# Attention scores over 32-row groups of TensorE and probabilities turned by transposing transfers

## The reference

```python
scale = 384 ** -0.5
q = (x @ Wq.T).reshape(b, n, 12, 32)
k = (x @ Wk.T).reshape(b, n, 12, 32)
v = (x @ Wv.T + bv).reshape(b, n, 12, 32)
scores = einsum('bqhd,bkhd->bhqk', q, k) * scale + (adj + adj)[:, None]
p = softmax(scores)                      # rows of zeros give 0
out = einsum('bhqk,bkhd->bqhd', p, v).reshape(b, n, 384)
return out @ Wo.T + bo
```

## Time and profile before

| | us |
|---|---|
| median of 3 runs | 1612.74 |
| lowest to highest | 1612.06 to 1613.54 |
| the profiled execution | 1610.95 |
| its span, first to last instruction | 1608.7 |
| PE busy | 1530.1 |
| DVE busy | 1247.8 |
| ACT busy | 900.9 |
| POOL busy | 470.3 |

### The profile page before, as it was taken

The page is one execution under the profiler, slowest core; times in us unless marked ns, Lnnn a source line. Parts: engine busy times, 40 slices in busy tenths (PEclk is TensorE's granted clock), DMA queues, the critical chain, the costliest instruction groups (busy, mean ns, idle before and its releaser), DMA issues.

```text
span 1608.7 us, 38829 instructions
## 1 busy us (share of the span) xinstructions
PE 1530.1 (95%) x13760; PEld 1501.6 (93%) x13760; DVE 1247.8 (78%) x4559; ACT 900.9 (56%) x2091; POOL 470.3 (29%) x926
## 2 busy tenths in 40 slices
PE   4799999999999999999999999999999999999984
PEld 4799999999999999999999999999999999999973
DVE  6568887778887777888777888777788877788753
ACT  4556566556556555656655665655565665566531
POOL 4113332233323223333223332313333322332222
PEclk8799999999999999999999999999999999999986
DMA  8222022222112222212222211222221222221100
GB/s 246 61 63 71 31 51 73 70 73 73 49 39 63 74 70 73 67 30 55 74 70 73 73 44 44 64 71 72 73 65 30 57 73 70 74 73 35 40 10 10
DMA packets 84637, 101.66 MB, mean 63 GB/s; under 512 B 6640, under 2 KB 84208, under 8 KB 84448
## 3 DMA queue, kind: packets, MB, share of 16 engines
q1 hardware_dynamic: 83872, 98.20, 22.6%
q0 software_dynamic: 576, 0.99, 0.3%
HBM read 61.41 MB, written 37.75 MB: 62 GB/s over the span
## 4 chain that ended last, share of the span: by engine, by line
PE 90%; ACT 5%; DVE 2%; issue 1%; DMA 1%; POOL 1%; SPq 0%; DVEq 0%; ACTq 0%; POOLq 0%
PE bank L355 72%; PE bank L430 5%; PE bank L361 4%; PE bank L423 3%; PE bank L414 3%; ACT c_sb L556 3%; PE bank L436 1%; ACT qk L495 1%; PE bank L448 0%; DMA pT<-w 0%; DMA k<-qk_parts 0%; ACT prob L519 0%; DMA x_sb<-x 0%; DVE c_sb L645 0%; DVE weights L582 0%
## 5 line engine op out<-in xcount | busy, mean ns | idle before, releaser
L355 PE MATMUL bank<-h,weights 128*128 128x256 f32 x3456 | 429.8, 282 | 5.4 <-DVE h L758 5.0
L355 PEld LDWEIGHTS bank<-h,weights 128*128 128x128 f32 x3456 | 412.4, 190 | 6.4 <-issue 5.7
L519 ACT ACTIVATE prob<-prob,rmin 128x128 f32<-128x128 f32 x768 | 240.3, 390 | 13.3 <-DVE rmin L675 13.3
L355 PE MATMUL bank<-weights,h 128*128 128x384 f32 x1152 | 228.7, 343 | 0.0
L355 PE MATMUL bank<-hA,weights 128*128 128x256 f32 x1728 | 218.8, 281 | 1.5 <-DVE hA L606 1.5
L606 DVE TENSOR_TENSOR n<-bank,n 128x512 fp32r<-128x512 f32 x192 | 128.5, 683 | 109.9 <-ACT n L495 109.8
L355 PEld LDWEIGHTS bank<-hA,weights 128*128 128x128 f32 x1728 | 210.9, 189 | 1.9 <-DVE hA L606 1.9
L355 PEld LDWEIGHTS bank<-weights,h 128*128 128x128 f32 x1152 | 193.9, 188 | 0.0
L817 POOL TENSOR_SCALAR less_mean_gnn<-mv_gnn 128x2 f32<-128x2 f32 x64 | 14.4, 225 | 582.0 <-DVE mv_gnn L611 582.0
L495 ACT ACTIVATE n<-bank 128x512 fp32r<-128x512 f32 x192 | 113.9, 594 | 117.6 <-PE bank L355 117.6
L675 DVE CUSTOM_DVE_ANT_0 prob<-bank,adj_sb 128x128 f32<-128x128 f32 x768 | 174.5, 286 | 0.1
(11 more groups left out here) (109 smaller groups left out, 2660.3 us busy)
## 6 DMA issues: line engine op xcount, KB each, us to landing
qk_parts<-qk SPq DMA_DIRECT2D x96, 256.0 KB, 2.4
q<-qk_parts SPq DMA_DIRECT2D x96, 192.0 KB, 4.6
k<-qk_parts SPq DMA_DIRECT2D x96, 192.0 KB, 5.5
x_sb<-x SPq DMA_DIRECT2D x32, 384.0 KB, 4.1
out<-x SPq DMA_DIRECT2D x32, 384.0 KB, 2.5
adj_sb<-adj SPq DMA_DIRECT2D x32, 128.0 KB, 2.1
prob<-w SPq DMA_DIRECT2D x4, 576.0 KB, 7.2
x<-w SPq DMA_DIRECT2D x3, 576.0 KB, 4.8
```

The source lines that it names most:

```text
L355: mm = pe.matmul(out, lhsT, rhs, start=(n == 0), stop=(n == len(pairs) - 1))
L519: e = act.activation(prob[:, j, h, :], prob[:, j, h, :], ACT.Exp, bias=rmin[:, j, h:h + 1], scale=-1.0)
```

## The change

- `q3`, `k3`, `qk_dram` and the steps qs and stack are gone. A score is now a product of 32 rows, read straight from `qk`, which holds two groups. The four heads of a chunk lie on the four row groups of the array, and the three parts are three products that add up in PSUM. S is now numbered by row group a instead of chunk: bank `Sja` gets the three heads a, 4 + a, 8 + a. All 36 products of a graph are issued in one step (`last == HC - 1`), in the order chunk, part, row group; the other S steps on PE only wait for their bank.
- The P steps are gone from PE, and their banks. `prob` holds one graph. ACT copies the high part of three heads in fp16 to a new tile `pp` (`ph`), DVE subtracts it from `prob` into its low half (`pl`), and SP turns three 128x128 blocks at a time from `pp` to `pT` (`pth`, `ptl`): 16 transfers a group. The same waits on PV0 and PV1 stand ahead of them.
- `xn1` has a tile of its own. `BANK` and `ORDER` are new for all engines: PV1 and its followers come late in a round, OT1 and WO1 in the next.

```diff
     "SP": [
-        ("k3", 1), ("ld_adj", 2), ("out", -1), ("qs0", 2), ("qs1", 2), ("qs2", 2), ("ld_x", 3), ("q3", 2)],
+        ("ld_x", 2), ("pth01", 1), ("pth03", 1), ("pth00", 1), ("pth02", 1), ("ptl01", 1), ("ptl03", 1), ("ptl02", 1),
+        ("ptl00", 1), ("ld_adj", 2), ("pth13", 1), ("pth11", 1), ("pth10", 1), ("ptl13", 1), ("ptl10", 1), ("ptl11", 1),
+        ("ptl12", 1), ("pth12", 1), ("out", -1)],
...
-        qk = sb("qk", [P, 2, 2 * C, T], F16)
+        qk = sb("qk", [P, 2, 2, 2 * C, T], F16)
+        xn1 = sb("xn1", [P, G, H])
         v2 = sb("v2", [P, 2, G, NH, DA], F16)
-        prob = sb("prob", [P, G, NH, P])
+        prob = sb("prob", [P, NH, P])
+        pp = sb("prob_parts", [P, 2, NH, P], F16)
         pT = sb("pT", [P, 2, NH, P], F16)
...
+                elif step[:2] == "pt":
+                    part, j, a = "hl".index(step[2]), int(step[3]), int(step[4])
+                    hs = slice(a * C, (a + 1) * C)
+                    if g == 0:
+                        sp.wait_ge(s_wlo, NW)
+                    sp.wait_ge(s_part[part][a], G * g + j + 1)
+                    if j == 0:
+                        wait_filled(sp, "PV1", g - 1)
                     else:
+                        wait_filled(sp, "PV0", g)
+                    sp.dma_start_transpose(pT[:, part, hs, :], pp[:, part, hs, :].rearrange("p h q -> p (h q)")).then_inc(s_turned[part][a], 16)
...
                 elif step[0] == "S":
-                    for a in range(HC):
-                        mm = pe.matmul(bank(step)[:, a * P:(a + 1) * P], q3[:, a * C + c, j * P:(j + 1) * P], k3[:, a * C + c, j * P:(j + 1) * P], start=True, stop=True)
-                    mm.then_inc(full(step), 1)
+                    j, last = int(step[1]), int(step[2])
+                    if last == HC - 1:
+                        for k in range(3):
+                            wait_drained(pe, f"QK{k}", g)
+                        js = slice(j * P, (j + 1) * P)
+                        for c in range(C):
+                            for n, (u, v) in enumerate(PARTS):
+                                for a in range(HC):
+                                    rs = slice(a * D, (a + 1) * D)
+                                    mm = pe.matmul(bank(f"S{j}{a}")[:, c * P:(c + 1) * P], qk[rs, g % 2, u, c, js], qk[rs, g % 2, v, C + c, js],
+                                                   start=(n == 0), stop=(n == len(PARTS) - 1))
+                                    if (c, n) == (C - 1, len(PARTS) - 1):
+                                        mm.then_inc(full(f"S{j}{a}"), 1)
                 elif step[:2] == "PV":
                     j = int(step[2])
                     wait_drained(pe, f"V{j}", g)
-                    for c in range(C):
-                        wait_drained(pe, f"P{j}{c}", g)
+                    for part in (HI, LO):
+                        for a in range(HC):
+                            pe.wait_ge(s_turned[part][a], 16 * (G * g + j + 1))
...
-                    for a in range(HC):
-                        mm = pe.transpose(bank(step)[:, a * P:(a + 1) * P], prob[:, j, c * HC + a, :], ident[:, :])
...
+                elif step[:2] == "ph":
+                    j, a = int(step[2]), int(step[3])
+                    act.wait_ge(s_exp[j][a], g + 1)
+                    ge(act, s_turned[HI][a], 16 * (G * g + j))
+                    act.activation(pp[:, HI, a * C:(a + 1) * C, :], prob[:, a:NH:HC, :], ACT.Copy).then_inc(s_part[HI][a], 1)
...
-                elif step[0] == "P":
-                    j, c = int(step[1]), int(step[2])
-                    hs = slice(c * HC, (c + 1) * HC)
-                    lo(step, g, pT[:, LO, hs, :], pT[:, HI, hs, :], HC * P, "p (h q) -> p h q", h=HC)
+                elif step[:2] == "pl":
+                    j, a = int(step[2]), int(step[3])
+                    hs = slice(a * C, (a + 1) * C)
+                    dve.wait_ge(s_part[HI][a], G * g + j + 1)
+                    ge(dve, s_turned[LO][a], 16 * (G * g + j))
+                    dve.tensor_tensor(pp[:, LO, hs, :], prob[:, a:NH:HC, :], pp[:, HI, hs, :], ALU.subtract).then_inc(s_part[LO][a], 1)
```

More of the change, by code:

```diff
@@ L71 @@
 BANK = {
[L72 to L79, removed]
+    0: ["N10", "U1", "S03", "N02", "T1b", "QK0"],
+    1: ["V0", "S12", "C01"],
+    2: ["N11", "T2b", "HL11", "HL00", "PV0", "PV1"],
+    3: ["OT1", "S02", "S10"],
+    4: ["HTa", "T2a", "N01", "S13", "HL01", "OT0"],
+    5: ["HL10", "S01", "C10", "AT", "T1a", "QK1", "WO0"],
+    6: ["HTb", "WO1", "N12", "N00", "U0", "QK2"],
+    7: ["S00", "C11", "S11", "C00", "V1"],
 }
@@ L83 @@
     "SP": [
[1 row of a table removed]
[3 rows of a table added]
     "PE": [
[5 rows of a table removed]
-    "ACT": [
[5 rows of a table removed]
-        ("HTb", 0)],
-    "DVE": [
[9 rows of a table removed]
[5 rows of a table added]
+    "ACT": [
[6 rows of a table added]
+    "DVE": [
[9 rows of a table added]
     "POOL": [
-        ("ln1", 2), ("ml", 0), ("gn1", -1), ("mu", 0), ("za0", -1), ("za1", -1), ("zb0", -1), ("xbo1", 2), ("xbo0", 2),
-        ("zb1", -1), ("gn0", 0), ("ln2", 1)],
-}
-SPLIT_JOBS = (["T1a", "T1b", "QK0", "QK1", "QK2", "V0", "V1"] + [f"P{j}{c}" for j in range(G) for c in range(C)] +
-              ["OT0", "OT1", "T2a", "T2b"] + [f"N{l}{k}" for l in range(L) for k in range(3)] +
+        ("ln2", 0), ("ln1", 2), ("xbo1", 2), ("xbo0", 2), ("ml", 0), ("gn1", -1), ("mu", 0), ("za0", -1), ("za1", -1),
+        ("zb0", -1), ("zb1", -1), ("gn0", 0)],
+}
+SPLIT_JOBS = (["T1a", "T1b", "QK0", "QK1", "QK2", "V0", "V1",
+              "OT0", "OT1", "T2a", "T2b"] + [f"N{l}{k}" for l in range(L) for k in range(3)] +
               [f"HL{l}{j}" for l in range(L) for j in range(G)])
@@ L218, in build @@
         s_xbo = [sem(f"x_plus_bo{j}") for j in range(G)]
-        s_q3, s_k3 = sem("q3_in"), sem("k3_in")
-        s_qs = [sem(f"qk_out{k}") for k in range(3)]
-        s_exp = [[sem(f"exps{j}{c}") for c in range(C)] for j in range(G)]
+        s_exp = [[sem(f"exps{j}{a}") for a in range(HC)] for j in range(G)]
+        s_part = [[sem(f"prob_{n}{a}") for a in range(HC)] for n in ("hi", "lo")]
+        s_turned = [[sem(f"prob_turned_{n}{a}") for a in range(HC)] for n in ("hi", "lo")]
         s_stats = {k: sem(f"stats_{k}") for k in ("ln1", "ln2")}
@@ L300, in load_weights @@
                     sp.dma_start(staged(m), w_d[m].rearrange("(c p) o -> p c o", p=P)).then_inc(s_wload[STAGE_OF[m]], 16)
-            def stack(dst, s, which, parts, p):
-                for r, part in enumerate(parts):
-                    heads = qk_dram[p, :, part, which * C:which * C + C, :].rearrange("(a d) c t -> d a (c t)", d=D)
-                    sp.dma_start(dst[D * r:D * r + D, :, :].rearrange("d (a c) t -> d a (c t)", a=HC), heads).then_inc(s, 16)
             def run(step, g):
@@ L418, in run @@
                     wait_drained(pe, f"V{j}", g)
-                    for c in range(C):
-                        wait_drained(pe, f"P{j}{c}", g)
+                    for part in (HI, LO):
+                        for a in range(HC):
+                            pe.wait_ge(s_turned[part][a], 16 * (G * g + j + 1))
                     for h in range(NH):
                         for n, (a, b) in enumerate(PARTS):
-                            mm = pe.matmul(bank(step)[:, h * DA:(h + 1) * DA], pT[:, a, h, :], v2[:, b, j, h, :],
+                            mm = pe.matmul(bank(step)[:, h * DA:(h + 1) * DA], pT[:, a, h % HC * C + h // HC, :], v2[:, b, j, h, :],
                                            start=(h == 0 and n == 0), stop=(n == 2), skip_group_check=True)
-                    mm.then_inc(full(step), 1)
-                elif step[0] == "P":
-                    j, c = int(step[1]), int(step[2])
-                    pe.wait_ge(s_exp[j][c], g + 1)
-                    for a in range(HC):
-                        mm = pe.transpose(bank(step)[:, a * P:(a + 1) * P], prob[:, j, c * HC + a, :], ident[:, :])
                     mm.then_inc(full(step), 1)
@@ L501, in run @@
                     act.wait_ge(s_ln["ln1"], g + 1)
-                    for k in range(3):
-                        ge(act, s_qs[k], 16 * g)
                     act.activation(xn1[:, j, :], x_sb[:, p, j, :], ACT.Relu, bias=shift["ln1"][:, j:j + 1], scale=scale["ln1"][:, j:j + 1]).then_inc(s_xn1[j], 1)
@@ L666, in run @@
                 elif step[0] == "S":
-                    j, c = int(step[1]), int(step[2])
+                    j, a = int(step[1]), int(step[2])
                     dve.wait_ge(s_adjin[p], 16 * (n + 1))
@@ L670, in run @@
                         dve.wait_ge(s_wlo, 8)
+                    ge(dve, s_part[LO][a], G * g + j)
                     wait_filled(dve, step, g)
-                    take_wait(3 + j * C + c)
-                    for a in range(HC):
+                    take_wait(3 + j * HC + a)
+                    for c in range(C):
                         h = c * HC + a
```

(6 more changed lines are left out.)

59 lines of the change are left out of this document (14 added, 45 removed), and 39 rows, old and new, of the table ORDER.

## The result

The changed kernel takes **1,723.5 us** (median of four runs, 1,721.2 to 1,726.4) against 1,613.1 us before on the same chip (four runs, 1,612.1 to 1,614.5). The ratio is **1.069, interval 1.067 to 1.070**: slower by 110 us, where 1,554 us and a gain of 59 were forecast. The time lies inside the range, on the side of rival 1, and the direction came out the other way.

A forecast was written before the change was run, and what follows sets the result against it. PE, busy 95% with hardly a gap, was taken as the bound. 1,610.95 us, -67 for PE's products, +8 for the ends, 1.8 for the median gave 1,554 us; range 1,528 to 1,760, the forecast's own 1,528 to 1,600.

The forecast's parts named there:

- rival 1: SP's queue before PV0 and PV1: transposing transfers too slow, gain gone at 1.13 us each, 1,675 us at 1.25; chance 0.32.
- t = 0.8 us: SP's queue: time one transposing transfer takes it, 0.42 us issue plus 0.36 us bytes, bounded by 0.42 and 1.66.
- 8t + L: Eight transfers before PV0 or PV1 plus the last one's tail: 8.5 us, fitting the covers, so no steady wait.
- The packet argument for rival 1: Transfers on SP's queue: 384 packets each, 24 per engine at 69 ns, giving 1.66 us a transfer.
- The landing, L = 2.1: Tail of the last transposing transfer before PV0 or PV1, taken from the adj load: 2.1 us.
- The covers of 9.5 and 10.9 us: PE's work that hides the transfers: 9.5 us between PV0 and PV1, 10.9 us from the first copies to PV0.
- Score products at 0.0253 us: 72 new 32-row products a group on PE, priced like PV's: +1.82 us; ends 0.0135 (side by side) and 0.054 each.
- Rival 2: Score products on PE: row groups don't overlap, 0.054 us each eats the whole gain, 1,620 us; chance 0.08.
- Removing the transposes and the old score products: PE, per group: 24 transposes of P go, -2.61 us, and 24 score products over 96 rows, -1.29 us.
- The swap of waits: PE: 0.3 us of wait appears at WO0 and about as much goes at HTb; counted as even.
- Rival 3: DVE's new subtractions from two SBUF tensors held up by POOL: 1.5 to 2.5 us on PE, 1,618 us; chance 0.08.
- The ends, +8 us: Filling and draining: nothing covers the first group's transfer chain; +8 us, 0 to 15.

The follow-up runs named there:

- plain_copy: The changed kernel with its 512 transposing transfers replaced by plain copies of the same size, output not the reference's: 1,549.5 us, ratio 0.961.
- six_blocks: The changed kernel with 8 transposing transfers of six blocks a group instead of 16 of three, whole computation kept: 1,551.2 us, ratio 0.962.
- six_serial: six_blocks with the score products issued row group by row group instead of in turn over the four: 1,596.3 us, ratio 0.989.

## Why the prediction went wrong, step by step

- **What bounds the kernel before: right.** PE with hardly a gap set the time, and in the two kernels without regular waits at PV (plain_copy, six_blocks) it sets it again, at 94% busy and a period of 45.56 and 45.50 us. The forecast was 45.5, though by two errors that cancel (below).
- **The failed step: t = 0.8 us for a transposing transfer.** It was built as 0.42 (a plain issue) plus 0.36 (98 KB at the rate of the plain queue). Measured: 1.21 us of issue and 1.30 from one to the next. Both halves were wrong in kind. The issue of a transposing transfer isn't that of a plain one (0.50 here), and the bytes add nothing to it, since SP is free again before they have moved. The bounds, 0.42 and 1.66, held the value, and rival 1 named the place, the formula and the break-even at t = 1.13, which lies under 1.30. What was missing was weight: the cover was exceeded by a value in the middle of the bounds, and 0.32 was too little for it. So the step "8t + L = 8.5 us, inside the covers, no wait" failed; the rows show 12.8 us from PV0 to PV1 and 4.26 us of wait a group.
- **The packet argument for rival 1** reached its number by a wrong road. Transfers do have 384 packets, but 69 ns a packet, taken from large rows, doesn't carry over: the packets of 256 bytes take 20 ns of an engine each (247 us of sixteen engines for 196,608).
- **The landing, L = 2.1: right** (2.3). **The covers of 9.5 and 10.9 us: right**; the rows above show 9.4 us at the first and, from the first issue for graph 0 at 804.72 to the end of PE's work at 815.47, 10.75 at the second. The formula of the waits is near the measurement (5.0 and 4.26 us a group), in part by luck: an issue counted twice stands for the handovers and the long issues.
- **Score products at 0.0253 us: too dear.** They take 0.017 with all around them, so 72 cost 1.22 us, not 1.82. The reason given (loads of 128 columns set the pace, as in PV) fell. Their pace inside a graph, 13.5 ns, is the lower end, 0.0135; what the forecast had no term for is the change to and from them (below). The order of the products, row group and bank together, is worth 45 us against six_serial. Rival 2 fell, and its own price of 0.054 was too high as well (0.042).
- **Removing the transposes and the old score products: nearly right.** In the same stretch of before as the earlier trace rows they took 2.57 and 1.26 us a group (2.61 and 1.29 predicted).
- **The swap of waits (0.46 at HTa for 0.3 at WO0): right** where PV doesn't wait. six_blocks shows `[0.36 <-DVE oT L595]`, and its rows have no regular wait at HTa.
- **Rival 3: fell.** The new subtractions take 549 ns on average, 0.55 predicted. One of the 256, with 1,347 ns, lies beside an instruction of POOL (L846); all others are below 0.57 us.
- **The ends, +8 us: right.** Beyond 32 periods before has 85.8 us, six_blocks 94.2, the changed kernel 93.9.
- **Not priced: the clock.** The rival's 51 us for each 0.1 us of t counted the wait and not the slower products behind it, 43 us in all by their rows, some 50 with all that grew beside the waits. With t = 1.30 and L = 2.3 the rival's formula gives 1,554 + 160 = 1,714 us. Cheaper score products take 19 away, the wait that is neither at HTa nor at WO0 15, the shorter waits at PV 24; the slower work adds 50 and the remainder below 14: 1,720, against 1,723.5. This sum was made after the fact, with measured terms.

The period as a sum: before 47.59; products of PE -2.61 (1.22 for 3.83 us); the wait at HTa -0.46; waits at PV +4.26; slower work behind them +1.6. That is 50.4, measured 50.80. In six_blocks the same sum is 47.59 - 2.61 - 0.46 + 0.18 + 0.32 = 45.02, measured 45.50. Both lack some 0.45 us a group, 14 us of the run. This is the error that hid the cheaper score products in the forecast of 45.5: luck. One piece of it can be seen where PE changes to the score products. Before, the two products of AT take 0.14 us to the next start, now 0.31 (808.34 to 808.65, above):

```profile
798.40 0.38 PE L448 MATMUL bank<-ident,adj_sb 128*128 128x128 f32 x2
798.54 0.76 PE L355 MATMUL bank<-weights,h 128*128 128x384 f32 x3
```

The starts of single products show that a change to 32-row products costs time, and a change back too. From the last product of HL to the first score product it is 0.271 us, where a 96-row one followed after 0.180 in the kernel before; from the last transpose of AT it is 0.204, where the last transposes before a 96-row product or a PV take 0.109. From the last score product to the next job it is 0.144, before 0.028. The three values are the same in six_serial (0.271, 0.204, 0.144), so the order of the score products doesn't matter to them. The two changes to 32 rows are 0.19 us a group of the missing 0.45; the changes back are already in the 1.22. The rest lies at other handovers, the transposes of OT above all (1.29 us a group from start to start against 1.07) and QK (6.44 against 6.30), and why is open.

The two figures that the prediction cited from the Trainium skill can now be judged. "VectorE: DVE Perf Modes" (The three transpose paths) gives 1.309 us for a 128x128 block. The trace agrees with that as a price of one instruction (1.18 us of issue for one block and 1.28 from one to the next, 1.30 for three) and not as a price of a block. "Advanced Engine Details and Errata" (X-Bar Transpose), transposing transfers as fast as plain ones, does not hold here: the queue needs 1.21 us to issue one against 0.50, and the engines 247 us for all of them against 148.

## What to carry to other kernels

Price a transfer by what it holds its queue for, per instruction, apart from its bytes and its landing. If the trace has no instruction of that kind, treat the gap between the bounds as the forecast's main risk, and measure that one number before building on it. Then make few, large instructions: the same change with half as many transposing transfers turned +6.9% into -3.8%.

A short wait of TensorE can cost more than its length when it recurs: in the changed kernel the products behind more than half of the waits at PV1 ran at a lower clock. And a wait of 0.3 us may be what keeps a longer chain hidden: look for what becomes late next before removing it.

## What the runs showed of the hardware

- A transposing transfer from SBUF to SBUF holds SP for 1.18, 1.21 and 1.22 us with one, three and six blocks of 128x128 fp16, against 0.50 us for a plain copy of three. It lands 2.3 us after the start of its issue (2.8 with six blocks, 2.0 for the plain copy).
- It moves in packets of 256 bytes. 196,608 of them took 247 us of the sixteen engines (290 us in transfers of six blocks); the same bytes in a plain copy, 148 us.
- 32-row fp16 products with 128 columns, in turn over four row groups into four banks: four start within 11 ns, and four every 56 ns. With the change to other products 36 take 0.61 us, 0.017 each; nine and nine on one row group and bank 0.042; those of 96 rows before, 0.054.
- The first 32-row product starts 0.09 us later behind 128-row ones than a 96-row one did, and the first 128-row product behind it 0.12 us later (0.144 against 0.028).
- Behind a wait of 1.73 us TensorE's granted clock fell to 0.67 over 3 us and 0.82 over the next 4. Behind 19 of 32 waits at PV1 the next products were slower, behind 13 they were not, and the two sets overlap in length. Idle products in the waits brought the run's clock from 0.943 to 0.977 and shortened it by 35 us; the slower products had cost some 43.
